# Slots stage of a two-layer kernel: four attention blocks side by side, the norm's gain and shift applied during the transposed copy

## The reference, cut to what matters

```python
q = S_new @ wq + bq
k = S_new @ wk + bk
v = S_new @ wv + bv
attn = softmax(einsum('bsq,btq->bst', q, k) * scale)
S_comm = einsum('bst,btd->bsd', attn, v)
y = S_new + S_comm
mu = y.mean(-1); var = y.var(-1)
y = (y - mu) * rsqrt(var + 1e-05) * ln_g + ln_b
slot_values = y @ wvp + bvp
out = einsum('bts,bsd->btd', alpha, slot_values) @ wo + bo
```

## Time and profile before

| | |
|---|---|
| median of 3 runs | 3036.32 us (3035.73 to 3037.11) |
| the profiled execution | 3052.64 us, its span from first to last instruction 3050.9 us |
| busy over the span | PE 2739.9 us, DVE 2085.3 us, ACT 1571.5 us, POOL 1542.0 us |
| TensorE's granted clock, mean | 0.932 of full |

### The profile page before, as it was taken

One profiled execution on the slowest core, in us unless ns is written; L12 is line 12 of the kernel. 1 busy time (PEld: TensorE's weight loads), 2 busy tenths in 40 slices (PEclk: granted clock), 3 DMA queues, 4 the chain that ended last, 5 costly groups with the idle time before them and its releaser, 6 DMA issues. The chain is left out here.

```text
span 3050.9 us, 43504 instructions
## 1 busy us (share of the span) xinstructions
PE 2739.9 (90%) x15650; PEld 2323.1 (76%) x15650; DVE 2085.3 (68%) x4205; ACT 1571.5 (52%) x3080; POOL 1542.0 (51%) x1155
## 2 busy tenths in 40 slices
PE   6789988886966599999999999999999999799698
PEld 5677777774533399898998989989899898677476
DVE  4776666652346677777777777777777777577655
ACT  2333333331212467777777777777777777111175
POOL 2454444431001256666666666666666666365545
PEclk9899999996877599999999999999999999899799
DMA  5211111112317823323233232332323313578464
GB/s 181 54 50 54 54 54 53 40 33 96 124 69 248 335 61 82 99 71 103 67 82 99 71 103 67 82 99 71 103 67 82 97 47 127 185 247 285 168 245 170
DMA packets 184385, 337.21 MB, mean 111 GB/s; under 512 B 52361, under 2 KB 58508, under 8 KB 177102
## 3 DMA queue, kind: packets, MB, share of 16 engines
q1 hardware_dynamic: 161937, 259.40, 28.7%
q0 software_dynamic: 11680, 45.02, 4.0%
q10 hardware_dynamic: 10560, 30.08, 2.5%
HBM read 166.39 MB, written 148.71 MB: 103 GB/s over the span
## 5 line engine op out<-in xcount | busy, mean ns | idle before, releaser
L1720 POOL TENSOR_SCALAR pa_Pr<-pa_Pr,pa_rs 128x590 f32<-128x590 f32 x512 | 902.8, 1768 | 547.4 <-DVE pa_rs L1951 547.2
L1955 DVE TENSOR_REDUCE pa_least<-pa_S 128x1 f32<-128x590 f32 x512 | 391.2, 764 | 207.0 <-PE pa_S L1785 204.7
L1907 DVE TENSOR_TENSOR pa_PTl<-pa_W,pa_PTh 128x512 fp32r<-128x512 f32 (+1 forms) x640 | 421.2, 684 | 30.8 <-ACT pa_PTh L1845 24.1
L1875 ACT ACTIVATE pa_Pr<-pa_S,pa_least 128x590 f32<-128x590 f32 x512 | 384.8, 752 | 81.8 <-DVE pa_least L1955 78.4
L1845 ACT ACTIVATE pa_PTh<-pa_W 128x512 fp32r<-128x512 f32 (+1 forms) x640 | 367.4, 596 | 83.9 <-PE pa_W L1796 64.7
L1796 PE MATMUL pa_W<-pa_ident,pa_Pr 128*128 128x128 f32 (+1 forms) x2560 | 368.1, 275 | 1.2 <-DVE pa_U L1907 0.6
L1796 PEld LDWEIGHTS pa_W<-pa_ident,pa_Pr 128*128 128x128 f32 (+1 forms) x2560 | 305.8, 143 | 25.9 <-POOL pa_Pr L1720 2.9
L1810 PE MATMUL pa_O<-pa_PTh,pa_V 128*128 128x512 f32 (+1 forms) x640 | 289.1, 452 | 17.7 <-DVE pa_PTl L1907 13.5
L1811 PE MATMUL pa_O<-pa_PTl,pa_V 128*128 128x512 f32 (+1 forms) x640 | 254.4, 397 | 0.0
L1783 PE MATMUL pa_S<-pa_U,pa_Qh 128*128 128x296 f32 (+1 forms) x1024 | 227.1, 303 | 0.2
L1785 PE MATMUL pa_S<-pa_Um,pa_Ql 128*128 128x296 f32 (+1 forms) x1024 | 223.3, 299 | 0.0
(11 more groups left out here) (469 smaller groups left out, 6849.0 us busy)
## 6 DMA issues: line engine op xcount, KB each, us to landing
xs_s<-pa_Ql SPq DMA_DIRECT2D x57, 576.0 KB
pa_Um<-pa_U SPq DMA_DIRECT2D x128, 147.5 KB
pa_Qh<-pa_Qh SPq DMA_DIRECT2D x128, 128.0 KB
o_s<-pa_O_hi SPq DMA_DIRECT2D x64, 256.0 KB, 2.0
o_s<-pa_O_lo SPq DMA_DIRECT2D x64, 256.0 KB, 2.3
Wkv_hi<-o_s SPq DMA_DIRECT2D x8, 2048.0 KB, 14.9
Wkv_lo<-o_s SPq DMA_DIRECT2D x8, 2048.0 KB, 19.5
z_s<-la_z_hi ACTq DMA_DIRECT2D x8, 1180.0 KB, 7.3
```

The costliest lines, as they stand in the source:

```text
L1720: pool.tensor_scalar(p, p, rs[:, g % 2, t:t + 1], None, ALU.mult).then_inc(*pool_s.mark("probs", n))
L1875: act.activation(Pr[g % 2][:, t, :], scored[n % 2], ACT.Exp, scale=-1.0, bias=least[:, g % 2, t:t + 1], accum_out=rs[:, g % 2, t:t + 1]).t ...
L1907: dve.tensor_tensor(out, src, f32(hi_ap), ALU.subtract).then_inc(*dve_s.mark(*name))
L1955: dve.tensor_reduce(least[:, g % 2, t:t + 1], scored[n % 2], AX, ALU.min).then_inc(*dve_s.mark("least", n))
```

## The change

The four blocks are taken step by step instead of one after the other: all four scores, all maxima, then all reciprocals and scalings, all transposes, all copies, all y. The PSUM units are listed in the new order. GpSimd makes rstd for each block by itself, as soon as its statistics are there. The norm on the rows is now only the subtraction and the multiplication by rstd (L1268 of the new kernel); g and b are applied in the copy of the transposed result, where a feature lies on a partition and both are one number per partition (L1273). For this g and b are loaded as 128x4 tiles straight from the plain vectors, with element (p, c) taken from place c * 128 + p; they are waited for apart, ahead of the yT copies. ACT's stream is the same but for the loads.

```diff
--- before.py
+++ after.py
@@ -968,7 +968,8 @@
         S0T = sb("S0T", [P, C, NS])
         bih, bhh = sb("bih", [P, 3 * C]), sb("bhh", [P, 3 * C])
         bq, bk, bvp = sb("bq", [P, 1]), sb("bk", [P, 1]), sb("bvp", [P, C])
-        bv_bc, g_bc, b_bc = (sb(n, [P, D]) for n in ("bv_bc", "g_bc", "b_bc"))
+        bv_bc = sb("bv_bc", [P, D])
+        g_col, b_col = sb("g_col", [P, C]), sb("b_col", [P, C])
         si = sb("si", [P, NP, D])
         siT = sb("siT", [P, C, BS])
         gh = sb("gh", [P, 3 * C, NS])
@@ -996,8 +997,7 @@
         units = [("gh", n) for n in range(3)] + [("siT", c) for c in range(C)]
         units += [("gi", c, n) for c in range(C) for n in range(3)]
         units += [("q",), ("k",)] + [("v", j) for j in range(NP)]
-        for j in range(NP):
-            units += [("A", j), ("AT", j), ("y", j)]
+        units += [(name, j) for name in ("A", "AT", "y") for j in range(NP)]
         units += [("yT", c) for c in range(C)] + [("sv", c) for c in range(C)] + [("vo", j) for j in range(NP)]
         banks = Banks(bank, units)
         dve_s.alias(("read", "q"), ("q",))
@@ -1020,7 +1020,7 @@
 
         parts = [("Wq", Wq, 0), ("Wq", Wq, 1)] + [("Wkv", Wkv, h) for h in range(4)]
         part_in, cut_hi, cut_lo = [sem(f"part{n}_in") for n in range(3)], sem("cut_hi"), sem("cut_lo")
-        copied = sem("copied")
+        copied, g_in = sem("copied"), sem("g_in")
         stage = lambda n: WihT[:, :, n % 3 * D:(n % 3 + 1) * D]
         kept = [(n, stage(n)[:, c:c + 2, :], t[0][:, c:c + 2, h * D:(h + 1) * D], t[1][:, c:c + 2, h * D:(h + 1) * D])
                 for n, (_, t, h) in enumerate(parts) for c in range(0, C, 2)]
@@ -1029,9 +1029,7 @@
 
         smalls = [(bih[:, :], a["L0_ffn_bih"]), (bhh[:, :], a["L0_ffn_bhh"]),
                   (bq[:, :], a["L0_ffn_bq"]), (bk[:, :], a["L0_ffn_bk"]), (bvp[:, :], a["L0_ffn_bvp"]),
-                  (bv_bc[:, :], a["L0_ffn_bv"].partition_broadcast(P)),
-                  (g_bc[:, :], a["L0_ffn_ln_g"].partition_broadcast(P)),
-                  (b_bc[:, :], a["L0_ffn_ln_b"].partition_broadcast(P))]
+                  (bv_bc[:, :], a["L0_ffn_bv"].partition_broadcast(P))]
 
         @block.sync
         def _(sp):
@@ -1062,10 +1060,12 @@
             make_identity(pool, ident, setup)
             pool.memset(minus_half[:, :], -0.5).then_inc(setup, 1)
             pool.memset(A[:, :, :], 0.0).then_inc(setup, 1)
-            pool.wait_ge(*dve_s.at(0, "var"))
-            pool.tensor_scalar(rstd[:, :], mv[:, :, 1], EPS, None, ALU.add).then_inc(*pool_s.mark("ve"))
-            pool.wait_ge(*pool_s.at(0, "ve"))
-            pool.tensor_tensor(rstd[:, :], rstd[:, :], minus_half[:, :], ALU.pow).then_inc(*pool_s.mark("rstd"))
+            for j in range(NP):
+                n = slice(j, j + 1)
+                pool.wait_ge(*dve_s.at(0, "var", j))
+                pool.tensor_scalar(rstd[:, n], mv[:, j, 1:2], EPS, None, ALU.add).then_inc(*pool_s.mark("ve", j))
+                pool.wait_ge(*pool_s.at(0, "ve", j))
+                pool.tensor_tensor(rstd[:, n], rstd[:, n], minus_half[:, n], ALU.pow).then_inc(*pool_s.mark("rstd", j))
 
         @block.tensor
         def _(pe):
@@ -1147,6 +1149,8 @@
             act.sem_inc(act_s.sem, act_s.per)
             for dst, src in smalls:
                 act.dma_start(dst, src).then_inc(small, 16)
+            for dst, name in ((g_col, "g"), (b_col, "b")):
+                act.dma_start(dst[:, :], a["L0_ffn_ln_" + name].rearrange("(c p) -> p c", p=P), allow_slow_non_contiguous=True).then_inc(g_in, 16)
             act.wait_ge(small, 16 * len(smalls))
 
             def kept_hi(n):
@@ -1243,30 +1247,31 @@
                 m.then_inc(*dve_s.mark("max", j))
                 dve.wait_ge(*dve_s.at(0, "max", j))
                 dve.tensor_scalar(amx[:, j:j + 1], amx[:, j:j + 1], -SCALE, None, ALU.mult).then_inc(*dve_s.mark("amx", j))
+            for j in range(NP):
                 dve.wait_ge(*act_s.at(0, "A", j, 1))
                 dve.reciprocal(asum[:, j:j + 1], asum[:, j:j + 1]).then_inc(*dve_s.mark("rsum", j))
                 dve.wait_ge(*dve_s.at(0, "rsum", j))
                 dve.tensor_scalar(A[:, j, :], A[:, j, :], asum[:, j:j + 1], None, ALU.mult).then_inc(*dve_s.mark("A", j))
+            for j in range(NP):
                 copy(("AT", j), AT[:, j, :])
+            for j in range(NP):
                 kept_lo(6 + j)
                 dve.wait_ge(*pe_s.at(0, "y", j))
                 dve.tensor_tensor(y[:, j, :], banks["y", j][:, :], bv_bc[:, :], ALU.add).then_inc(*dve_s.mark("y+bv", j))
                 dve.wait_ge(*dve_s.at(0, "y+bv", j))
                 dve.bn_stats(stats[:, j, :], y[:, j, :]).then_inc(*dve_s.mark("stats", j))
                 dve.wait_ge(*dve_s.at(0, "stats", j))
-                m = dve.bn_aggr(mv[:, j, :], stats[:, j, :])
-            m.then_inc(*dve_s.mark("var"))
-            dve.wait_ge(*dve_s.at(0, "var"))
-            dve.wait_ge(*pool_s.at(0, "rstd"))
+                dve.bn_aggr(mv[:, j, :], stats[:, j, :]).then_inc(*dve_s.mark("var", j))
             for j in range(NP):
+                dve.wait_ge(*dve_s.at(0, "var", j))
+                dve.wait_ge(*pool_s.at(0, "rstd", j))
                 dve.tensor_scalar(y[:, j, :], y[:, j, :], mv[:, j, 0:1], rstd[:, j:j + 1], ALU.subtract, ALU.mult)\
-                   .then_inc(*dve_s.mark("normed", j))
-                dve.wait_ge(*dve_s.at(0, "normed", j))
-                dve.tensor_tensor(y[:, j, :], y[:, j, :], g_bc[:, :], ALU.mult).then_inc(*dve_s.mark("*g", j))
-                dve.wait_ge(*dve_s.at(0, "*g", j))
-                dve.tensor_tensor(y[:, j, :], y[:, j, :], b_bc[:, :], ALU.add).then_inc(*dve_s.mark("yn", j))
+                   .then_inc(*dve_s.mark("yn", j))
+            dve.wait_ge(g_in, 32)
             for c in range(C):
-                copy(("yT", c), yT[:, c, :])
+                dve.wait_ge(*pe_s.at(0, "yT", c))
+                dve.tensor_scalar(yT[:, c, :], banks["yT", c][:, :], g_col[:, c:c + 1], b_col[:, c:c + 1], ALU.mult, ALU.add)\
+                   .then_inc(*dve_s.mark("yT", c))
             for n in range(6 + NP, len(kept)):
                 kept_lo(n)
             for c in range(C):
```

## The result

The change is faster: median 3019.33 us of five runs (3015.26 to 3025.77) against 3036.32 us of five runs of before (3034.4 to 3037.11), a ratio of 0.9947 with a 95% interval of 0.9932 to 0.9961, so 17.0 us less, between 11.8 and 20.6. The forecast was 3018.1 us with a range of 3014 to 3024. The profiled execution of the change took 3020.18 us (span 3018.4 us, granted clock 0.939).

What follows compares the result with a forecast made beforehand. No engine bounds the slots stage; the chain of steps through its attention blocks does. Savings of 11.4 (order) + 6.9 (norm) - 0.1 (copy) = 18.2 us, taken from the median 3036.32 us, gave 3018.1 us, range 3014 to 3024.

Steps and rivals of the forecast that it cites:

- Maxima and exponentials side by side: Slots stage's attention blocks: ACT sets the pace at 1.91 us a block; block 3's scaling 7.4 us behind the first maxima.
- Piece 8: ACT's weight piece ahead of block 3, needing weight part 4: a new wait, covered with 3.6 us to spare.
- Transposes and copies, the first y: Slots stage: first y starts 8.4 us behind the first maxima, and DVE has it at 12.2 us.
- The four y: PE's y run: clock rises inside the second y, DVE then paces at 2.78 us a block; 11.4 us saved.
- rival 1: Clock stays low through all y, PE paces at 3.44 us, 9.4 us saved there: 3020.1 us; chance 0.17.
- The norm: Last statistics to last normed rows: 2.4 us instead of 9.3, 6.9 us saved; ends 2.2 and 3.3 us.
- Rival 2: GpSimd is locked out in the norm while DVE works: 0.9 us less gain, 3019.0 us; chance 0.12.
- Gain and shift in the copy: Copies of the transposed result: each perhaps a tenth longer than 0.69 us, only the last on the path; -0.1 us.
- The loads: Small loads of g and b: 0.034 us a packet, 3.1 us more on the queues, covered; cost 0.
- sv's clock, "luck, I take 0": sv's start: whether it catches the full clock 2 us earlier or later is luck; counted as 0.
- The profiled execution: Whole kernel: profiled 3052.64 us against median 3036.32, since a profiled run is longer everywhere; same saving subtracted from the median.
- Rival 5: Side-by-side order brings nothing, in-order streams still tying blocks to the previous y; only the norm gains: 3029.5 us; chance 0.03.

Runs made afterwards that it cites:

- e3: The change with ACT's four weight pieces moved from between the exponentials to behind all of them; 3016.95 us in one run.
- e4: The change with DVE's four weight pieces moved from ahead of each y's addition to behind the copies of the transposed result; 3018.53 us in one run.
- e5: The change with ten more loads in 4-byte packets, 5120 packets, right behind those of g and b; 3033.13 us in one run.
- e8: The change itself once more, on another chip; median 3028.4 us, ratio to before 0.9934.
- e9: e1 with PE kept busy in the norm by matmuls whose result the transposes overwrite; 3029.18 us in one run.
- e10: e1 once more, on the same chip as e9; 3025.19 us in one run.
- e2: The change with the old block-by-block order put back, so the new norm alone; median 3032.09 us, ratio to before 0.9983.
- e1: The change with the old norm put back, so the side-by-side order alone; median 3027.95 us, ratio to before 0.9966.

## Why the prediction was right, point by point

The forecast mechanism is what happened, and the total was off by 1.2 us. That closeness is partly luck: the trace has 2.8 us more from the first maxima on than the forecast's 18.2, and the medians 1.2 less. By its own steps:

- *Maxima and exponentials side by side.* Expected were 1.91 us a block and block 3's scaling at t + 7.4. It was 1.93 us and 854.71 - 847.19 = 7.52. e3 showed that ACT's pieces set this pace. Piece 8 held nothing up.
- *Transposes and copies, the first y.* t + 8.4 expected, 8.28 measured; DVE had it at 12.07 instead of 12.2.
- *The four y.* The clock rose inside the second y, as read from block 0, and rival 1 is out. DVE paced, with 2.66 us instead of 2.78: the next instruction starts about 0.1 us before the piece's row ends, so adding 1.22 us left the overlap out. Three such paces make 0.36 us, and with the two steps above the last statistics came at 21.67 instead of 22.1. Saved 11.8 instead of 11.4.
- *The norm.* 2.05 us instead of 2.4, saved 7.24 instead of 6.9. GpSimd lost only 0.22 us to each of its two instructions; the 0.38 us doubled, from the latents row, was too much, and the answer was covered, as at the prediction's lower end. The worse end, by which GpSimd gets nowhere while DVE works, did not come: both of its instructions ran while DVE's row went on, each 0.2 us longer. So the prediction read the Trainium skill's rule ("SBUF — State Buffer", "Who interferes with whom") too widely; what it holds off is one instruction for the length of another, not for a whole row. Beside a piece of 1.2 us the loss is 0.88 us (1.10 against 0.22 in e4), but there nobody waits for it. Rival 2 is out.
- *Gain and shift in the copy.* -0.1 expected; from the end of the norm to the last copy it is 3.86 us instead of 3.82. A copy takes 0.81 us where the plain one takes 0.69, more than the tenth that was allowed, and three of the four wait for nothing now, while before each waited 0.16 us for PE.
- *The loads.* Cost 0 was right, but the working behind it was not. There is no 3.1 us on the queues: by e5 a small packet takes 0.010 us of an engine, and 128 of them per engine 1.3 us, which is what the two broadcasts had taken (16 x 0.081). The earlier trace rows were used as if the rest of the stretch were filled with small packets; that only bounds the price from above. The same row has the better reading: 6.6% of 16 engines over 1.2 us for 146 small packets is 0.009 us each.
- *sv's clock, "luck, I take 0".* This is the step that failed, by 1.9 us. It was put down as luck, and e8, e9 and e10 show that it repeats with the kernel and follows what PE does ahead of sv. In the change the pause behind the last y is 4.4 us and the clock still dips (0.88, then 0.55), but it is back at 1.00 when sv starts at 874.87 us. With either part alone the half level still covers sv's start (e2 has 0.50 from 880 to 889 us, and sv starts at 887.02). Why the level comes back at 874 us in the change and not later is not settled by these runs.
- *The profiled execution.* "A profiled run is longer everywhere" was wrong. Before's one execution was 12.0 us longer than the change's in the experts stage alone; the twelve executions have that stage between 426 and 441 us, and the change's own profiled execution (3020.18 us) lies within 1 us of its median. Subtracting from the median was right all the same.
- *Sum.* 11.8 + 7.24 + 1.9 make 20.9 us in the trace from the first maxima on, against the forecast 18.2; the first chip's runs gave 17.0 (11.8 to 20.6), e8's chip 20.1 (15.2 to 25.3). On one chip the runs of a kernel scatter over up to 10.5 us, those of before over up to 15, so they cannot tell 18.2 from 20.9.

Rival 5, that the order brings nothing, is out by e1: nothing in the streams ties one block to the y of the one before.

## What to carry to other kernels

When no engine is busy and a chain of small steps is walked block by block, write the steps side by side, then look for bulk work of the same engine that stands between two steps of different blocks: here four pieces each on ACT and DVE, moved behind the chain, gave another 6 us in the trace. Count TensorE's pause ahead of a long run of matmuls as part of the price of whatever makes the pause: shortening the 9.3 us norm saved its own 7.2 us and, with the new order (not without it, by e2), 1.9 us more in matmuls that nobody had edited. For edits of 10 us in 3000, compare stage by stage from a common event in the trace; the totals scatter by as much.

## What the runs showed of the hardware that was not expected

- 5120 added packets of 4 bytes made five bulk loads land 0.6 to 1.7 us later, and the first, of 3 MB, not at all, though 1634 of them passed beside it. Two queues passed packets one for one (1184 and 1187 in 7 us), at about 0.010 us for a small one. It is the small load that waits: 10.3 and 15.4 us for 2 KB.
- A GpSimd instruction on one column takes 0.22 us alone and 1.10 us beside a DVE subtraction of two 128x1024 SBUF operands; beside DVE instructions of 0.53 us it takes 0.44. DVE's own instructions showed no loss: the norm's subtraction takes 0.54 us in the change and before, where GpSimd was idle, and the piece 1.19 us beside GpSimd and 1.22 us without.
- Idle PE time has a price at the next matmuls. With 7.5 us of pause (and three of 1.4 us) 13 transposes took 1.4 us longer and sv 2.7 us; filling the pauses with matmuls that are thrown away gave 3.6 us back without any other edit (e10 and e9, one execution each, 69.56 and 65.94 us from the first maxima to the next stage).
